# Two transformer-like layers on one core: expert work per block of 128 rows in two shared banks, two banks for the scores S, and an order offset for every step

## The chip, the cores and the metric

The kernel runs on one core of one Trainium2 chip. The metric is the time of one launch on the device in microseconds (us). Three runs of the kernel before gave a median of 2736.35 us (2729.3 to 2741.03).

## The reference

The input x is 16 batches of 512 rows and 128 channels, all float32. Two layers follow each other; each computes a mixing part `s` and a gating part `g` and adds their product:

```
xn = layernorm(x)
x  = x + mix(xn) * silu(experts(xn))
```

In layer 0 the mixing part is an RWKV time mix: five small low-rank mixes, projections r, k, v, g, a decay w, a linear recurrence over 512 positions for 2 heads of 64 channels, a group norm and an output projection. The expert part picks the best 2 of 8 experts for each row and sums their outputs, weighted by a softmax:

```
h1 = x @ W1[e].T ; h2 = x @ W2[e].T          # 128 -> 256
y  = (h1 * sigmoid(h1) * h2) @ W3[e].T       # 256 -> 128
```

In layer 1 the mixing part is softmax attention over 512 positions with 16 heads of 8 channels. The expert part again picks 2 of 8 experts (the gate is a sigmoid, applied to the input rows) and adds a ninth expert, the shared one, that every row passes through.

## The kernel before

**Engines and order.** Each step of the computation is a tuple `(n, layer, kind, ...)` for batch n. `due_times()` (L138) writes a due time for each step of an even and an odd batch, in microseconds relative to the start of the batch; `due()` (L255) adds PERIOD = 150.23 for each batch. `order(engine)` (L333) sorts all steps by due time plus one offset for each engine and kind, `LATER` (L124). Each engine runs its part of each step in that order, strictly. A due time thus sets only the order; the time at which work runs is set by semaphores. The work of several batches and of both layers is interleaved in that one order.

**Experts.** Rows of two batches are sorted by expert into NB = 23 blocks of 128 rows. SP loads three weight tiles for each block (`weights`, into a ring of WRING = 4). TensorE (PE) transposes four blocks at a time (`xT`). A unit of work is a pair of blocks, one every UNIT_EVERY = 10.7 us of due time: `up` writes four 128x128 products (2 blocks x 2 halves of the hidden width) into bank h, `gate` four into bank g (L711 to L728), and `down` writes two products, each a sum over two halves, into bank y (L729 to L750). ScalarE (ACT) takes tanh of bank h (L984), VectorE (DVE) multiplies with bank h and then with bank g (L1329, L1337). After every second pair ACT copies bank y, four blocks, to SBUF in one instruction (`yout`, L992), and SP stores it. The shared expert is two units of 512 rows, one for each half of the hidden width: `up` and `gate` are each one matmul of 512 columns (L719). Its `down` is eight matmuls of 128 columns (L741) and ACT copies it out in one instruction (`shared`, L997).

**Attention.** For each of 16 heads and 4 query blocks, `smax` writes the scores S of 128 queries and 512 keys to bank s (L887), and DVE takes the row maximum (L1445). Later the transposed scores minus the maximum go to bank st (`soft`, L902), and ACT takes exp into `probs` (L1063). `pv` multiplies with v (L916). The bias rows of the keys, which add the maximum, come from the instruction that copies the keys (`keys`, L1046, with a bias column).

**PSUM.** There are eight banks of 128x512 float32: mix and attn (all other work of layer 0 and layer 1), h, g, y, s, st and pv. `room()` makes PE wait until the bank that it is about to fill has been emptied, `content()` makes a reader wait until it has been filled.

```
            def room(s, b, i=0):
                if fill(s, b, i) > 1:
                    pe.wait_ge(emptied[b], fill(s, b, i) - 1)
                return bank[b]
```

**POOL** does elementwise work of layer 0 and the indirect DMAs that scatter rows to blocks and gather them back. It is not edited, but its order is.

Of the kernel before, what the change touches and what calls it, by code (L numbers as in the profile page):

```python
# [23 lines left out]
F32 = mybir.dt.float32  # L24
# [3 lines left out]
ALU = mybir.AluOpType  # L28
# [22 lines left out]
PAIRS, QUADS = (NB + 1) // 2, (NB + 3) // 4  # L51
HALF, FIRST = (PAIRS + FT) // 2, 8
# [31 lines left out]
GATE_AFTER = 3.13  # L84
DOWN_AFTER = 9.35
# [38 lines left out]
LATER = {'dve': {'keys': -0.95, 'decays': -1.98, 'gate': 0.4, 'norm': -0.45, 'weights': -0.86, 'cross128': -0.06, 'soft': -0.63, 'xT': 1.23, 'down': -2.14, 'mrow': 0.36, 'cross512': -0.24, 'scatter': -1.18, 'combine': -0.18, 'fetch': 0.58, 'outT': -0.02, 'yout': -0.28, 'value': 0.32, 'up': 0.06, 'decay': 0.75, 'finish': 0.7, 'wkvsum': 0.41, 'attnv': -3.03, 'normx': 0.61, 'yn': -0.01, 'diag': 0.22, 'proj': 0.52, 'shared': -0.39, 'pair': -1.16, 'cross256': -2.03, 'normT': 1.49, 'gather': 0.51, 'qk': -0.52, 'wkvT': 0.16, 'stack': 0.68, 'place': -0.69, 'mixed': 0.23, 'smax': -0.5, 'rank': -0.55, 'wkv': 0.06, 'weigh': -0.09, 'lora': -0.01, 'route': -0.07, 'mixin': -0.02, 'headsT': -0.17, 'pv': 0.53}, 'act': {'combine': -2.74, 'finish': 0.06, 'norm': -0.45, 'normx': -1.63, 'wkvT': 0.51, 'decay': 0.05, 'place': -1.66, 'outT': 0.85, 'down': -1.04, 'mrow': 0.28, 'normT': 0.35, 'route': 0.83, 'weights': -0.01, 'rank': 1.59, 'decays': -0.17, 'value': -0.08, 'lora': 1.09, 'wkv': -0.19, 'pair': -0.92, 'scatter': 1.57, 'smax': -2.19, 'cross256': -1.14, 'level': -2.39, 'mixed': 0.75, 'gate': 1.56, 'weigh': -0.63, 'headsT': 1.65, 'keys': 0.0, 'fetch': 0.93, 'cross128': 0.52, 'wkvsum': 1.0, 'yout': -0.63, 'shared': -0.22, 'attnv': 0.09, 'yn': -0.68, 'stack': 0.23, 'mixin': -0.02, 'gather': 0.09, 'diag': 1.25, 'cross512': -0.29, 'proj': 0.48, 'up': -0.0, 'xT': -0.03}, 'pool': {'xT': -0.33, 'combine': 0.06, 'cross512': -1.35, 'yn': -0.4, 'decay': -1.18, 'normx': -0.81, 'wkvT': 0.01, 'place': -0.48, 'attnv': 0.31, 'cross128': -0.93, 'fetch': -0.7, 'shared': 1.29, 'gate': 0.02, 'proj': -2.38, 'up': -1.17, 'mrow': -1.39, 'pv': -1.28, 'decays': -0.35, 'cross256': -0.02, 'qk': -0.22, 'soft': -0.4, 'diag': 1.02, 'lora': 1.06, 'stack': -0.02, 'yout': 0.94, 'weights': 1.23, 'mixed': -1.93, 'route': -0.07, 'mixin': -1.35, 'normT': -0.75, 'rank': 0.28, 'down': -1.25, 'finish': -0.92, 'scatter': -1.12, 'wkvsum': 0.13, 'outT': 0.11, 'pair': 0.13, 'norm': -0.24, 'smax': -2.87, 'level': -0.19, 'keys': 0.14, 'weigh': -0.21, 'wkv': -1.48, 'value': -0.18, 'gather': -0.21}, 'pe': {'wkvT': 0.16, 'outT': 0.36, 'decay': 0.03, 'cross512': -1.89, 'decays': 0.61, 'pv': 0.31, 'normx': -2.94, 'cross256': -0.05, 'gather': 0.77, 'proj': -0.06, 'down': -1.15, 'xT': -0.05, 'pair': 0.29, 'norm': 0.32, 'lora': -0.74, 'cross128': -0.29, 'mixin': 2.35, 'headsT': 0.35, 'place': 1.83, 'yout': 0.68, 'combine': 1.77, 'soft': -0.04, 'weigh': -1.08, 'fetch': -1.68, 'wkvsum': -0.26, 'normT': 0.17, 'mixed': 0.21, 'gate': -0.06, 'yn': 0.7, 'up': -0.14, 'value': -0.74, 'keys': 1.89, 'diag': 0.74, 'qk': 0.02, 'attnv': -0.64, 'rank': -0.03, 'shared': -0.84, 'mrow': 0.17, 'route': 0.18, 'wkv': -0.79, 'weights': 2.03, 'scatter': -0.45, 'finish': -0.51, 'level': -0.32}, 'sp': {'smax': 0.64, 'pv': -0.29, 'attnv': -0.42, 'scatter': 0.19, 'xT': -0.1, 'place': -1.05, 'headsT': 1.02, 'normx': 0.27, 'yout': 1.14, 'normT': -0.09, 'level': -0.3, 'yn': 0.57, 'cross256': 2.02, 'combine': 0.02, 'rank': -0.15, 'cross128': 0.28, 'wkvsum': 0.6, 'fetch': 0.14, 'soft': 0.62, 'weights': -0.11, 'qk': 0.85, 'weigh': 0.25, 'decays': 0.36, 'wkvT': 0.24, 'outT': -0.0, 'up': 1.39, 'diag': 0.2, 'wkv': -1.04, 'gate': -0.07, 'route': -2.12, 'mixin': 0.01, 'keys': 1.3, 'stack': -1.16, 'gather': 0.66, 'value': -1.01, 'mrow': -0.13, 'lora': -0.04, 'pair': -0.13, 'shared': -0.03, 'mixed': 0.26, 'proj': -0.33, 'down': 0.15, 'cross512': 0.17}}  # L124


def pair_of(layer, u):

    return u - FT * layer if u >= FT * layer else None


def blocks_of(layer, u):

    p = pair_of(layer, u)
    return list(range(2 * p, min(2 * p + 2, NB)))


def due_times():  # L138
# [33 lines left out]
    for i in range(4 * HALF):  # L172
        at = UNIT_START + UNIT_EVERY * i
        j = i % (2 * HALF)
        if FIRST <= j < FIRST + FT:
            unit(odd if i < 2 * HALF else even, 1, j - FIRST, at + (PERIOD if i < 2 * HALF else 0.0))
        else:
            layer = int(i >= 2 * HALF)
            unit(even, layer, (j if j < FIRST else j - FT) + FT * layer, at + 2 * PERIOD * layer)
# [23 lines left out]
def unit(d, layer, u, at):  # L203

    d[layer, "up", u] = at
    d[layer, "gate", u] = at + GATE_AFTER
    p = pair_of(layer, u)
    if p is not None or u == FT - 1:
        d[layer, "down", u] = at + DOWN_AFTER
    if p is None:  # L210
        if u == FT - 1:
            d[1, "shared"] = d[1, "down", u] + YOUT_AFTER
        return
    for b in blocks_of(layer, u):
        d[layer, "weights", b] = at - WEIGHTS_BEFORE + 0.3 * (b % 2)
    if p % 2 == 0:
        d[layer, "xT", p // 2] = at - XT_BEFORE
    if p % 2 or p == PAIRS - 1:
        d[layer, "yout", p // 2] = at + DOWN_AFTER + YOUT_AFTER

# [24 lines left out]
HB, GB, YB, SB, TB, VB = "h", "g", "y", "s", "st", "pv"  # L245
BANKS = MISC + (HB, GB, YB, SB, TB, VB)
# [5 lines left out]
EXPERTS = ("weights", "xT", "up", "gate", "down", "yout", "shared")  # L252


def due(step):  # L255
# [19 lines left out]
    return PERIOD * n + at  # L275


def fills(step):

    n, layer, kind, *which = step  # L280
    if kind in ("up", "gate"):
        return [HB if kind == "up" else GB]
    if kind == "down":
        p = pair_of(layer, which[0])
        return [YB] if p is None or p % 2 == 0 else []
    if kind in ("smax", "soft"):

        if n == 0 and kind == "smax" and which[0] < HG and which[1] % 2:
            return [TB]
        if n == B - 1 and kind == "soft" and which[0] % 2:  # L290
            return [SB if which[0] >= NH - HG else MISC[0]]
        return [SB if kind == "smax" else TB]
    if kind == "pv":
        return [VB] if which[1] == 0 else []
    if kind in ("keep", "load", "mixed", "norm", "decays", "weights", "yout", "shared", "scatter", "fetch", "gather", "combine", "normx", "weigh", "place", "yn", "keys"):
        return []
    return [MISC[layer]] * (2 if kind in ("mixin", "decay") else 1)
# [3 lines left out]
UPS = [s for s in PLAN if s[2] == "up"]  # L301
DOWNS = [[s for s in PLAN if s[1:3] == (i, "down")] for i in (0, 1)]
# [20 lines left out]
def down_of(s):  # L323

    n, layer, _, u = s
    return (n, layer, "down", FT - 1 if pair_of(layer, u) is None else u)


def quad_fill(n, layer, m):

    return fill((n, layer, "down", 2 * m + FT * layer), YB)


def order(engine):

    return sorted(PLAN, key=lambda s: due(s) + LATER[engine].get(s[2], 0.0))


def two_layer_kernel(nc, x, cols, mix1, square, mix2, dec1, dec2, up0, gate0, down0, up1, gate1, down1,
                     routers, ident, masks, select, iota, out):  # L340
    with ExitStack() as ctx:
# [69 lines left out]
        hid = sb("hid", [P, HRING, T])  # L411
# [118 lines left out]
        th_done = sem("th_done")  # L530
        down_done = [sem(f"down_done{i}") for i in L]
# [25 lines left out]
        def _(sp):  # L557
# [62 lines left out]
            def weights(s):  # L620
# [5 lines left out]
                if i >= WRING:  # L626

                    old = LOADS[i - WRING]
                    down = (old[0], old[1], "down", old[3] // 2 + FT * old[1])
# [6 lines left out]
            def yout(s):  # L636
# [3 lines left out]
                sp.wait_ge(emptied[YB], quad_fill(n, layer, m))  # L640
# [10 lines left out]
        def _(pe):  # L651
# [23 lines left out]
            def step(s):  # L675
# [38 lines left out]
                elif kind in ("up", "gate"):  # L714
                    u, part = which[0], 0 if kind == "up" else 1
                    b = HB if kind == "up" else GB
                    if pair_of(layer, u) is None:
                        pe.wait_ge(emptied[MISC[1]], fill((n, 1, "normT"), MISC[1]))
                        mm(room(s, b)[:], shared_sb[:, part, u * P:(u + 1) * P], xnT1[:], start=True, stop=True).then_inc(filled[b], 1)  # L719
                    else:  # L720
                        ps = room(s, b)
                        for i, blk in enumerate(blocks_of(layer, u)):
# [8 lines left out]
                elif kind == "down":  # L731
# [4 lines left out]
                    if p is None or p % 2 == 0:  # L736
                        room(s, YB)
# [872 lines left out]
```

## Time and profile before

| What | Value |
|---|---|
| median of 3 runs | 2736.35 us |
| lowest and highest run | 2729.3 and 2741.03 us |
| span of the profiled execution | 2756.3 us |
| PE busy (matmuls) | 2327.5 us, 84% |
| PE busy (weight loads) | 1579.5 us, 57% |
| DVE busy | 1609.7 us, 58% |
| ACT busy | 1350.3 us, 49% |
| POOL busy | 1237.6 us, 45% |
| mean granted TensorE clock | 0.946 |

The profiled execution has no time of its own beside its span, from first to last instruction; that span is 20 us above the median of the runs, which were not profiled. Matmuls are pipelined and the profile models their ends, so that a matmul is counted busy for longer than it keeps the next one from starting: two matmuls of one queue overlap in the list. The weight loads (PEld) are a second row of the same engine.

### The profile page before, as it was taken

What the parts mean: (1) busy time and instruction counts of PE and PEld (TensorE: products, weight loads), DVE (VectorE), ACT (ScalarE), POOL (GpSimd) and SP (SyncE); (2) the same over time, 40 slices, a digit from 0 to 9 for tenths busy, and PEclk for the clock granted to TensorE, in tenths of its full rate; (3) what the DMA queues carried; (4) which work ended last, traced back from release to release, by engine and by line L of the source; (5) the groups of instructions that cost most, each with busy time, mean ns of one, the idle gap of its engine ahead of it and who ended that gap; (6) DMA issues with size and microseconds to landing.
All of it is one profiled execution on the core that took longest, in us unless ns stands there. A gap on an engine that the chain in (4) does not pass through costs nothing. (4 is left out here: it accounts for less than half of the span.)

```text
span 2756.3 us, 50388 instructions
## 1 busy us (share of the span) xinstructions
PE 2327.5 (84%) x16602; PEld 1579.5 (57%) x16602; DVE 1609.7 (58%) x3864; ACT 1350.3 (49%) x2485; POOL 1237.6 (45%) x1364
## 2 busy tenths in 40 slices
PE   1666889898998989898898989889898889998785
PEld 1553556566665656566565656556565656665363
DVE  2336465766657475665657465665647566665452
ACT  0222555455554546545554545545554555555453
POOL 3144435364633645444732646435643646323503
PEclk5768899999999999999999999999999999999897
DMA  3320223323333333323332333324333332321132
GB/s 104 111 75 12 68 91 95 106 73 111 98 100 89 99 99 99 94 77 111 101 103 82 99 93 97 107 75 121 100 90 93 96 102 85 110 72 41 53 107 68
DMA packets 308767, 248.27 MB, mean 90 GB/s; under 512 B 31040, under 2 KB 300064, under 8 KB 308512
## 3 DMA queue, kind: packets, MB, share of 16 engines
q1 hardware_dynamic: 292128, 211.46, 25.7%
q0 software_dynamic: 16384, 33.59, 4.1%
q8 instruction: 138, 2.26, 0.3%
q14 instruction: 117, 0.96, 0.1%
HBM read 195.77 MB, written 48.10 MB: 88 GB/s over the span
## 5 line engine op out<-in xcount | busy, mean ns | idle before, releaser
L1445 DVE TENSOR_REDUCE rowmax<-bank_s 128x1 f32<-128x512 f32 x1016 | 698.5, 687 | 565.6 <-PE bank_s L887 542.3
L1063 ACT ACTIVATE probs<-bank_st 128x512 f32<-128x512 f32 x992 | 589.4, 594 | 462.7 <-PE bank_st L902 431.9
L902 PE MATMUL bank_st<-qs,ks 128*128 128x512 f32 x992 | 512.6, 517 | 59.3 <-ACT probs L1063 58.0
L887 PE MATMUL bank_s<-ks,qs 128*128 128x512 f32 x1016 | 448.6, 442 | 93.8 <-DVE rowmax L1445 84.9
L1207 POOL DMA_INDIRECT yg<-ys_d,index x256 | 249.8, 976 | 260.7 <-issue 242.1
L902 PEld LDWEIGHTS bank_st<-qs,ks 128*128 128x128 f32 x992 | 191.5, 193 | 234.5 <-ACT probs L1063 140.6
L887 PEld LDWEIGHTS bank_s<-ks,qs 128*128 128x128 f32 x1016 | 197.0, 194 | 207.4 <-DVE rowmax L1445 173.6
L1329 DVE SCALAR_TENSOR_TENSOR hid<-hid,bank_h 128x512 f32<-128x512 f32 x224 | 148.6, 664 | 223.7 <-ACT hid L984 216.7
L916 PE MATMUL bank_pv<-probs,v 128*32 128x512 f32 x2048 | 253.8, 614 | 0.8 <-ACT probs L1063 0.8
L728 PEld LDWEIGHTS bank_h<-xT_sb,wbuf 128*128 128x128 f32 x1472 | 202.6, 202 | 27.9 <-issue 14.6
L1125 POOL TENSOR_TENSOR pause_sb<-ones_sb,power_sb 128x8 f32<-128x8 f32 x128 | 214.2, 1674 | 3.9
L728 PE MATMUL bank_h<-xT_sb,wbuf 128*128 128x128 f32 x1472 | 211.7, 288 | 4.6 <-DMA wbuf<-down 2.4
L728 PEld LDWEIGHTS bank_g<-xT_sb,wbuf 128*128 128x128 f32 x1472 | 195.0, 195 | 30.7 <-issue 20.0
L747 PEld LDWEIGHTS bank_y<-wbuf,hid 128*128 128x128 f32 x1472 | 193.8, 193 | 23.8 <-DVE hid L1337 7.1
L1146 POOL TENSOR_TENSOR xmixT<-moved,xnT 128x512 f32<-128x512 f32 x80 | 86.9, 1086 | 264.2 <-DVE moved L1367 259.7
L747 PE MATMUL bank_y<-wbuf,hid 128*128 128x128 f32 x1472 | 199.6, 278 | 4.2 <-DVE hid L1337 4.1
L728 PE MATMUL bank_g<-xT_sb,wbuf 128*128 128x128 f32 x1472 | 200.9, 279 | 0.0
L984 ACT ACTIVATE hid<-bank_h 128x512 f32<-128x512 f32 x224 | 130.2, 581 | 130.4 <-PE bank_h L728 121.7
L1046 ACT ACTIVATE ks<-bank_attn,cols_sb 32x512 fp32r<-32x512 f32 x256 | 173.7, 679 | 16.0 <-PE bank_attn L879 13.1
L1133 POOL TENSOR_TENSOR rstd<-vareps,power_sb 128x4 f32<-128x4 f32 x32 | 32.5, 1015 | 316.5 <-DVE vareps L1288 316.5
L1337 DVE TENSOR_TENSOR hid<-hid,bank_g 128x512 f32<-128x512 f32 x224 | 148.0, 661 | 28.7 <-PE bank_g L728 13.6
L1195 POOL DMA_INDIRECT xs_d<-xn,index x128 | 127.3, 995 | 61.7 <-DVE index L1555 31.6
(245 smaller groups left out, 3659.4 us busy)
## 6 DMA issues: line engine op xcount, KB each, us to landing
wbuf<-up SPq DMA_DIRECT2D x368, 128.0 KB
wbuf<-gate SPq DMA_DIRECT2D x368, 128.0 KB
wbuf<-down SPq DMA_DIRECT2D x368, 128.0 KB
xs_sb<-xs_d SPq DMA_DIRECT2D x80, 256.0 KB
ys_d<-y_sb SPq DMA_DIRECT2D x80, 256.0 KB
xn<-x SPq DMA_DIRECT2D x16, 256.0 KB, 3.2
x<-x SPq DMA_DIRECT2D x16, 256.0 KB, 4.1
yg<-ys_d,index POOLq DMA_INDIRECT x256
```

The lines of the kernel that those rows point to most:

```text
L728: last = mm(ps[:, (FT * i + f) * P:(FT * i + f + 1) * P], wbuf[:, load % WRING, part, f * P:(f + 1) * P], rows, start=True, stop=True)
L747: last = mm(bank[YB][:, blk % 4 * P:(blk % 4 + 1) * P], hid[:, NUMBER[n, layer, "up", u] % HRING, (FT * i + f) * P:(FT * i + f + 1) * P], ...
L887: mm(room(s, b)[:], qs[:, slot, q * P:(q + 1) * P], ks[:, slot, j, :], start=True, stop=True).then_inc(filled[b], 1)
L902: mm(room(s, b)[:], ks[:, slot, j, k * P:(k + 1) * P], qs[:, slot, :], start=True, stop=True).then_inc(filled[b], 1)
L916: last = mm(ps[32 * j:32 * j + 32, :], v1_all[:, k, (DK + 1) * (HG * g + j):(DK + 1) * (HG * g + j) + VCOLS], probs[:, slot, :], start=k = ...
L1046: last = A(ks[rows, (NG * n + g) % RING, j, :], content((n, 1, "stack", AK, g), misc)[rows, :], ACT.Identity, bias=cols_sb[rows, COL_KONE: ...
L1063: A(probs[:, tile % PRING, :], ps[:], ACT.Exp).then_inc(emptied[b], 1)
L1125: tt(pause_sb[:], ones_sb[:].to_broadcast([P, 8]), power_sb[:], ALU.pow).then_inc(rested, 1)
L1207: pool.indirect_dma_start(yg[layer][:, k, q, :], None, ys_d[layer][:, :], where).then_inc(gathered[layer], 16)
L1329: v.scalar_tensor_tensor(out=hid[:, i % HRING, 0:wide], in0=hid[:, i % HRING, 0:wide], scalar=1.0, in1=bank[HB][:, 0:wide], op0=ALU.add, o ...
L1337: v.tensor_tensor(hid[:, i % HRING, 0:wide], hid[:, i % HRING, 0:wide], ps[:, 0:wide], ALU.mult).then_inc(emptied[GB], 1)
L1445: v.reduce_max(rowmax[:, h // HG % 2, NT * (h % HG) + q:NT * (h % HG) + q + 1], content(s, b)[:], AX).then_inc(emptied[b], 1)
```

## The change

1. The expert unit is one block, one every 5.35 us of due time. Its `up` step writes all four products, up and gate, into one bank (columns 0 to 255 and 256 to 511). Its `down` step writes into the first 128 columns of the same bank once DVE has read both parts. Units take the banks e0 and e1 in turn. ACT copies each block's 128x128 result to SBUF by itself; `yout` is only the store. The shared expert becomes four units of 128 rows in the same form.
2. Banks h, g, y and s become e0, e1, s0 and s1. S alternates between s0 and s1 by query block.
3. `MOVED` adds an offset to each single step of a pair of batches (with further offsets for the first two and the last two batches), and `SHIFTED` an offset for each engine, layer and kind. `GATE_AFTER`, `DOWN_AFTER` and some entries of `LATER` change.
4. The bias rows of the keys are set to 1.0 once, by four memsets at the start. The key copies take 24 rows instead of 32 and have no bias column.

```diff
-GATE_AFTER = 3.13
-DOWN_AFTER = 9.35
+GATE_AFTER = 1.5
+DOWN_AFTER = 6.5
...
+        for k in range(2):
+            if first + k < NB + SHARED * layer:
+                unit(d, layer, first + k, at + k * UNIT_EVERY / 2)
...
-HB, GB, YB, SB, TB, VB = "h", "g", "y", "s", "st", "pv"
+EB, SB, TB, VB = ("e0", "e1"), ("s0", "s1"), "st", "pv"
...
-    return PERIOD * n + at
+    return PERIOD * n + at + moved(step)
+
+MOVED = (
+    {
+        (0, 0, "combine"): [0.23], (0, 0, "cross128"): [-2.17], (0, 0, "cross256"): [1.4], (0, 0, "cross512"): [0, -0.58], (0, 0, "decay"): [-2.67],
...
+        (0, 0, "yout"): [2.72, 1.08, -1.22, 0, -6.42, -14.1], (0, 1, "attnv"): [-0.49], (0, 1, "combine"): [0.39],
...
+def moved(step):
+    n = step[0]
+    i, still = PLACES[n % DUO][step[1:]]
+    return DRIFT * n + among(MOVED, n, (n % DUO, *step[1:3]), i, still)
+
+def shifted(engine, step):
+    every, *ends = SHIFTED[engine].get(step[1:3], (0, 0, 0))
+    return every + (ends[class_of(step[0]) - 1] if class_of(step[0]) else 0)
...
+    if kind in ("up", "down"):
+        return [EB[TURN[n, layer, which[0]] % 2]]
...
-        return [SB if kind == "smax" else TB]
+        return [SB[which[1] % 2] if kind == "smax" else TB]
...
 def order(engine):
-    return sorted(PLAN, key=lambda s: due(s) + LATER[engine].get(s[2], 0.0))
+    return sorted(PLAN, key=lambda s: due(s) + LATER[engine].get(s[2], 0.0) + shifted(engine, s))
...
+                    ps = room(s, b)
+                    for part in range(2):
+                        for f in range(FT):
+                            last = mm(ps[:, (FT * part + f) * P:(FT * part + f + 1) * P], w[:, part, f * P:(f + 1) * P], rows,
+                                      start=True, stop=True)
+                    last.then_inc(up_done, 1)
                 elif kind == "down":
...
+                    ps = room(s, b)
+                    for f in range(FT):
+                        last = mm(ps[:, 0:P], hid[:, turn_of(n, layer, u) % HRING, f * P:(f + 1) * P], w[:, 2, f * P:(f + 1) * P],
+                                  start=f == 0, stop=f == FT - 1)
                     last.then_inc(down_done[layer], 1)
...
+                    act.wait_ge(up_done, i + 1)
...
+                    A(hid[:, i % HRING, :], bank[fills(s)[0]][:, 0:FT * P], ACT.Tanh, scale=0.5).then_inc(th_done, 1)
+                elif kind == "down":
+                    act.wait_ge(down_done[layer], NUMBER[s] + 1)
...
+                    A(dst, bank[b][:, 0:P], ACT.Copy).then_inc(emptied[b], 1)
...
-                    rows = slice(32 * j, 32 * j + 32)
-                    last = A(ks[rows, (NG * n + g) % RING, j, :], content((n, 1, "stack", AK, g), misc)[rows, :], ACT.Identity,
-                             bias=cols_sb[rows, COL_KONE:COL_KONE + 1])
+                    rows = slice(32 * j, 32 * j + 3 * DK)
+                    last = A(ks[rows, (NG * n + g) % RING, j, :], content((n, 1, "stack", AK, g), misc)[rows, :], ACT.Copy)
...
+                    for j in range(HG):
+                        v.memset(ks[32 * j:32 * j + 32, :, j, :].bitcast(F32), 1.0).then_inc(s_late, 1)
```

## Rows read from the trace of the kernel before

**Rows 1.** The page: busy time and share of each engine.
```profile
PE 2327.5 (84%) x16602; PEld 1579.5 (57%) x16602; DVE 1609.7 (58%) x3864; ACT 1350.3 (49%) x2485; POOL 1237.6 (45%) x1364
```

**Rows 2.** The steady stretch as one window: busy us (instructions) of each engine.
```profile
450.00:2400.00 1950.00, 1742.56 (x12873) 1197.51 (x12871) 1232.12 (x2951) 1038.94 (x1922) 947.57 (x1040) 0.99 0.33 97
```

**Rows 3.** PE's waits, whole span: releaser, us in total, times, longest.
```profile
PE bank_s L887 <- DVE rowmax L1445: 84.9, 129, 1.8
PE bank_st L902 <- ACT probs L1063: 58.0, 102, 2.6
```

**Rows 4.** PE's waits within 450 to 2400 us.
```profile
PE bank_s L887 <- DVE rowmax L1445: 58.5, 88, 1.6
PE bank_st L902 <- ACT probs L1063: 39.7, 71, 0.8
```

**Rows 5.** Waits of the weight loads of the same two lines, whole span.
```profile
PEld bank_s L887 <- DVE rowmax L1445: 173.6, 257, 2.3
PEld bank_st L902 <- ACT probs L1063: 140.6, 201, 3.0
PEld bank_st L902 <- issue: 83.4, 163, 1.7
PEld bank_s L887 <- issue: 16.0, 53, 0.8
```

**Rows 6.** Timeline near 1207 us: start, duration, engine, instruction, idle before.
```profile
1207.07 0.39 PE L887 MATMUL bank_s<-ks,qs 128*128 128x512 f32 x1
...
1207.50 0.69 DVE L1445 TENSOR_REDUCE rowmax<-bank_s 128x1 f32<-128x512 f32 x1 [0.44 <-PE bank_s L887]
...
1207.92 0.63 PE L902 MATMUL bank_st<-qs,ks 128*128 128x512 f32 x1
1208.24 0.19 PEld L887 LDWEIGHTS bank_s<-ks,qs 128*128 128x128 f32 x1
1208.39 0.40 PE L887 MATMUL bank_s<-ks,qs 128*128 128x512 f32 x1
```

**Rows 7.** Timeline of PE: a 512-column matmul (two passes), then four 128-column ones.
```profile
1201.61 1.02 PE L719 MATMUL bank_g<-xnT,shared_sb 128*128 128x512 f32 x2
1202.07 0.80 PE L902 MATMUL bank_st<-qs,ks 128*128 128x512 f32 x1
...
1226.72 1.05 PE L747 MATMUL bank_y<-wbuf,hid 128*128 128x128 f32 x8
1227.53 0.48 PE L902 MATMUL bank_st<-qs,ks 128*128 128x512 f32 x1
```

**Rows 8.** Groups by line and form: the shared expert's first matmuls.
```profile
L719 PE MATMUL bank_h<-xnT,shared_sb 128*128 128x512 f32 x64 | 33.5, 605 | 0.0
```

**Rows 9.** Groups of ACT by form: busy us, mean ns, then idle before.
```profile
L1046 ACT ACTIVATE ks<-bank_attn,cols_sb 32x512 fp32r<-32x512 f32 x256 | 173.7, 679 | 16.0 <-PE bank_attn L879 13.1 <-issue 0.2
L984 ACT ACTIVATE hid<-bank_h 128x512 f32<-128x512 f32 x208 | 124.1, 597 | 127.8 <-PE bank_h L728 119.2 <-PE bank_h L719 6.0
L992 ACT ACTIVATE y_sb<-bank_y 128x512 f32<-128x512 f32 x80 | 47.3, 591 | 20.4 <-PE bank_y L747 18.9 <-issue 1.5
...
L1039 ACT ACTIVATE qs<-bank_attn 128x512 fp32r<-128x512 f32 x64 | 38.2, 597 | 63.8 <-PE bank_attn L879 59.0 <-issue 4.7
...
L984 ACT ACTIVATE hid<-bank_h 128x256 f32<-128x256 f32 x16 | 6.1, 381 | 2.6 <-PE bank_h L728 2.5
L1105 ACT ACTIVATE expd<-cum 128x128 f32<-128x128 f32 x16 | 4.8, 302 | 0.0
```

**Rows 10.** Groups of DVE by form: one expert product at two widths.
```profile
L1329 DVE SCALAR_TENSOR_TENSOR hid<-hid,bank_h 128x512 f32<-128x512 f32 x208 | 142.1, 683 | 218.5 <-ACT hid L984 211.5 <-issue 7.0
...
L1329 DVE SCALAR_TENSOR_TENSOR hid<-hid,bank_h 128x256 f32<-128x256 f32 x16 | 6.6, 411 | 5.2 <-ACT hid L984 5.2
```

**Rows 11.** Timeline of the start: the memset of the keys, and PE's wait.
```profile
106.99 5.18 DVE L1296 MEMSET ks<- 128x6144 f32 x1 [1.23 <-issue]
...
118.78 1.08 PE L712 MATMUL bank_mix<-ident_sb,xs_sb 128*128 128x128 f32 x4 [7.85 <-DVE moved L1367]
```

More of the change, by code:

```diff
@@ L138, in due_times, with block_of @@
+def block_of(layer, u):
+    return u - SHARED * layer if u >= SHARED * layer else None
 def due_times():
@@ L206, in unit @@
     d[layer, "gate", u] = at + GATE_AFTER
[L207 to L212, printed above, removed]
-        return
[L214 to L219, printed above, removed]
+    d[layer, "down", u] = at + DOWN_AFTER
+    b = block_of(layer, u)
+    if b is None:
+        return
+    d[layer, "weights", b] = at - WEIGHTS_BEFORE
+    if b % 4 == 0:
+        d[layer, "xT", b // 4] = at - XT_BEFORE
+    if b % 4 == 3 or b == NB - 1:
+        d[layer, "yout", b // 4] = at + DOWN_AFTER + YOUT_AFTER
 def attention(d, start):
@@ L251 @@
 PLACED_IN = ("route", "weigh", "place", "rank", "scatter", "fetch")
-EXPERTS = ("weights", "xT", "up", "gate", "down", "yout", "shared")
+EXPERTS = ("weights", "xT", "up", "gate", "down", "yout")
 def due(step):
@@ new lines, in class_of, with among @@
+def class_of(n):
+    return 1 if n < DUO else 2 if n >= B - DUO else 0
+def among(table, n, key, i, otherwise):
+    at = table[0].get(key, otherwise)[i]
+    return at + table[class_of(n)].get(key, otherwise)[i] if class_of(n) else at
+PLACES = [{} for i in range(DUO)]
+for places, steps in zip(PLACES, DUE):
+    for s in sorted(steps):
+        kin = [t for t in sorted(steps) if t[:2] == s[:2]]
+        places[s] = (kin.index(s), [0.0] * len(kin))
+def moved(step):
+    n = step[0]
+    i, still = PLACES[n % DUO][step[1:]]
+    return DRIFT * n + among(MOVED, n, (n % DUO, *step[1:3]), i, still)
@@ L290, in fills @@
         if n == B - 1 and kind == "soft" and which[0] % 2:
-            return [SB if which[0] >= NH - HG else MISC[0]]
-        return [SB if kind == "smax" else TB]
+            return [SB[0] if which[0] >= NH - HG else MISC[0]]
+        return [SB[which[1] % 2] if kind == "smax" else TB]
     if kind == "pv":
         return [VB] if which[1] == 0 else []
-    if kind in ("keep", "load", "mixed", "norm", "decays", "weights", "yout", "shared", "scatter", "fetch", "gather", "combine", "normx", "weigh", "place", "yn", "keys"):
+    if kind in ("keep", "load", "mixed", "norm", "decays", "weights", "gate", "yout", "scatter", "fetch", "gather", "combine", "normx", "weigh", "place", "yn", "keys"):
@@ L301 @@
 UPS = [s for s in PLAN if s[2] == "up"]
+TURN = {(s[0], s[1], s[3]): i for i, s in enumerate(UPS)}
 DOWNS = [[s for s in PLAN if s[1:3] == (i, "down")] for i in (0, 1)]
@@ L320, in fill, with turn_of @@
     return BEFORE[step, bank] + n + 1
[L323 to L331, printed above, removed]
+def turn_of(n, layer, u):
+    return TURN[n, layer, u]
 def order(engine):
-    return sorted(PLAN, key=lambda s: due(s) + LATER[engine].get(s[2], 0.0))
+    return sorted(PLAN, key=lambda s: due(s) + LATER[engine].get(s[2], 0.0) + shifted(engine, s))
 def two_layer_kernel(nc, x, cols, mix1, square, mix2, dec1, dec2, up0, gate0, down0, up1, gate1, down1,
@@ L639, in yout @@
                 i, count = NUMBER[s], min(4, NB - 4 * m)
-                sp.wait_ge(emptied[YB], quad_fill(n, layer, m))
+                last = (n, layer, "down", min(4 * m + 3, NB - 1) + SHARED * layer)
+                sp.wait_ge(emptied[fills(last)[0]], fill(last, fills(last)[0]))
                 if n > 0 and m == 0:
@@ L713, in step @@
                     last.then_inc(filled[misc], 1)
[L714 to L717, printed above, removed]
+                elif kind == "up":
+                    u = which[0]
+                    blk, b = block_of(layer, u), fills(s)[0]
+                    if blk is None:
                         pe.wait_ge(emptied[MISC[1]], fill((n, 1, "normT"), MISC[1]))
-                        mm(room(s, b)[:], shared_sb[:, part, u * P:(u + 1) * P], xnT1[:], start=True, stop=True).then_inc(filled[b], 1)
+                        w, rows = shared_sb, xnT1[:, u * P:(u + 1) * P]
@@ L720, in step @@
                     else:
-                        ps = room(s, b)
-                        for i, blk in enumerate(blocks_of(layer, u)):
-                            load, turned = NUMBER[n, layer, "weights", blk], (n, layer, "xT", blk // 4)
-                            pe.wait_ge(w_in[load % WRING], 48 * (load // WRING + 1))
-                            pe.wait_ge(emptied[misc], fill(turned, misc))
-                            rows = xT_sb[:, NUMBER[turned] % 2, blk % 4 * P:(blk % 4 + 1) * P]
-                            for f in range(FT):
-                                last = mm(ps[:, (FT * i + f) * P:(FT * i + f + 1) * P], wbuf[:, load % WRING, part, f * P:(f + 1) * P], rows,
-                                          start=True, stop=True)
@@ L730, in step @@
-                        last.then_inc(filled[b], 1)
+                        load, turned = NUMBER[n, layer, "weights", blk], (n, layer, "xT", blk // 4)
+                        pe.wait_ge(w_in[load % WRING], 48 * (load // WRING + 1))
+                        pe.wait_ge(emptied[misc], fill(turned, misc))
+                        w, rows = wbuf[:, load % WRING], xT_sb[:, NUMBER[turned] % 2, blk % 4 * P:(blk % 4 + 1) * P]
+                    ps = room(s, b)
[3 more added lines that the diff above has]
+                                      start=True, stop=True)
@@ L731, in step @@
+                    last.then_inc(up_done, 1)
                 elif kind == "down":
                     u = which[0]
-                    pe.wait_ge(emptied[GB], fill((n, layer, "gate", u), GB))
-                    p = pair_of(layer, u)
-                    if p is None or p % 2 == 0:
-                        room(s, YB)
-                    if p is None:
-                        for q in range(NT):
-                            for f in range(FT):
-                                last = mm(bank[YB][:, q * P:(q + 1) * P], hid[:, NUMBER[n, 1, "up", f] % HRING, q * P:(q + 1) * P],
-                                          shared_sb[:, 2, f * P:(f + 1) * P], start=f == 0, stop=f == FT - 1)
-                    else:
-                        for i, blk in enumerate(blocks_of(layer, u)):
-                            load = NUMBER[n, layer, "weights", blk]
-                            for f in range(FT):
-                                last = mm(bank[YB][:, blk % 4 * P:(blk % 4 + 1) * P],
-                                          hid[:, NUMBER[n, layer, "up", u] % HRING, (FT * i + f) * P:(FT * i + f + 1) * P],
-                                          wbuf[:, load % WRING, 2, f * P:(f + 1) * P], start=f == 0, stop=f == FT - 1)
@@ L750, in step @@
+                    blk, b = block_of(layer, u), fills(s)[0]
+                    w = shared_sb if blk is None else wbuf[:, NUMBER[n, layer, "weights", blk] % WRING]
+                    ps = room(s, b)
+                    for f in range(FT):
+                        last = mm(ps[:, 0:P], hid[:, turn_of(n, layer, u) % HRING, f * P:(f + 1) * P], w[:, 2, f * P:(f + 1) * P],
+                                  start=f == 0, stop=f == FT - 1)
                     last.then_inc(down_done[layer], 1)
```

235 lines of the change are left out of this document (185 added, 50 removed).

## The prediction

> **What bounds the kernel now.** I read the busy shares first. PE is busy 84% of the span of 2756.3 us, DVE 58%, ACT 49%, POOL 45% [rows 1]: PE is the engine to watch, and nothing else is near full. The steady stretch comes next, since the span holds a start and an end that the change touches little: of its 1950 us PE is busy 1742.6, so 207 us are idle [rows 2]. The list of PE's waits then says who ends the idle time. The first entry is the score matmul S, held by the row maximum on DVE because S has one bank: 84.9 us in 129 waits. The second is the transposed score matmul, held by exp on ACT: 58.0 us in 102 [rows 3]. In the steady stretch the two are 58.5 and 39.7 us, 98 of 207; the remaining 109 is spread over dozens of pairs of instructions [rows 4].
>
> PE's idle time understates these waits, because a matmul is counted busy while its end drains. For one, S starts at 1207.07, the maximum runs from 1207.50 to 1208.19, the next weight load of S comes at 1208.24 and the matmul at 1208.39 [rows 6]. PE waited for DVE there, yet its row shows no idle time, since the matmul of 1207.92 is drawn until 1208.55. The weight loads' waits show the other side: 173.6 us in 257 for S, 140.6 us in 201 for the transposed scores [rows 5]. These hold the time in which PE is streaming anyway. Where the loads of the same lines wait for nothing, the gap is 16.0/53 = 0.30 us for S and 83.4/163 = 0.51 us for the other. Taken off, 173.6 - 257 x 0.30 = 97 us and 140.6 - 201 x 0.51 = 38 us remain.
>
> All sums are made against the span of 2756.3 us. The runs' median is 2736.35, 20 us or 0.7% lower, without a profiler; a difference of some tens of us carries over unchanged.
>
> **1. A second bank for S.** S(k) now waits for the maximum of k-2, not k-1, so each wait shrinks by the distance of two S steps; at 64 a batch and a due-time period of 150 us this is 2.35 us, and the longest wait was 1.8 us (2.3 at the load) [rows 3, 5]. Nearly all go. Bounds of the gain: 84.9 (idle alone) to 173.6 us (all of the loads' waits). I take 105, near the 97 worked out above, with a little for waits of other steps behind a late S.
>
> **2. What is late next.** The transposed scores keep one bank. In the order they mostly stand beside an S, so a PE that no longer stops at S reaches them earlier, while ACT is no faster. Nothing returned is one end, all 105 the other. I take a quarter, +25: an exp of 0.6 us is followed in the plan by 2.35 us to the next, so most of the time is still there, but 201 of the loads did wait [rows 5].
>
> **3. The shared expert in blocks.** Before, a batch had four float32 matmuls of 512 columns (64 records of bank h are 16 batches x 2 units x 2 passes [rows 8], bank g as many). After, it has 16 of 128 columns. Start to start, the 512-column one took 1202.07 - 1201.61 = 0.46 us; four of 128 columns took 1227.53 - 1226.72 = 0.81 us, 0.20 each; by their drawn length of 1.05 us it would be 0.26, and I take 0.22 [rows 7]. 16 x 0.22 - 4 x 0.46 = 1.7 us a batch, x 16 = +27 us, all on PE: the weights are loaded four times as often. Bounds: 0 (hidden in waits that stay) to +37 (at 0.26). The routed experts keep their number of matmuls, only grouped differently: 0, ends -5 and +5 by the gap of 0.30 at a load.
>
> A 128-column pass thus takes about 0.11 us [rows 7], about as long as the load of its weights would leave. The Trainium skill (TensorE: Matmul & The Clock Gate, Back-to-back issue gap) gives, for an isolated matmul at the full clock, N/2.4 + 2.5 ns, which is 56 ns at N=128 and 216 at N=512. By that, a pass four times as narrow costs a quarter, and the split would be nearly free (an estimate from the page: 32 x 56 against 8 x 216 ns, +0.1 us a batch). The trace disagrees for this stream, and the rows decide.
>
> **4. More and smaller instructions on ACT and DVE.** Units go from 14 a batch to 27 (46 routed and 8 shared in two batches), 432 in all. ACT: tanh before 208 x 0.597 + 16 x 0.381 = 130 us, after 432 x 0.381 = 165, +35. Copies out: 80 and 32 more, all taken at 0.591, make 66 us; after, 432 of 128x128, no such row, nearest is the narrow exp of 302 ns: 130, +64. Keys: 256 x (0.679 - 0.597) = -21, the nearest copy without a bias being that of the queries. Together +78 us on an engine with half its time free [rows 1, 9]. DVE: two products a unit, 448 of 0.68 become 864 of 0.41: +58 us [rows 10]. Both lie beside PE's work, which covers them; what shows is that an exp sometimes stands behind one more copy. Bounds 0 and +78, taken +10, as the idle of ACT is eight times the addition. If the cover fails, this becomes the rival below.
>
> **5. The unit's bank.** A bank is held from `up` until the copy after `down`. Work alone: 0.9 + 0.38 + 2 x 0.41 + 0.46 + 0.30 = 2.9 us; in due times 6.5 plus the down and its copy, 7.3 us, against 10.7 us until its next turn. Slack 3.4 us: cost 0, ends 0 and +43 (a tenth of a microsecond for each of 432). DVE used to read bank h while PE wrote bank g; now ACT's tanh waits until all four products are there, about 0.45 us later; that is within the slack. The Trainium skill (PSUM — Partial Sum Buffer, PSUM bank collisions raise a hardware error) says that two engines may not touch one bank at once and want a semaphore by bank. That is the rule against this layout, since four steps of three engines must now take turns in it; no row of before shows a bank shared so. What it costs in time would be the holding time just given.
>
> **6. The memsets.** Four of 1536 elements a row beside one of 6144 in 5.18 us: +5.2 us on DVE at about 115 us. It is on the path: PE stood 7.85 us for the product behind those memsets [rows 11]. +5, ends 0 and +5.2.
>
> **7. The order.** Single steps move by up to some 3 us against their neighbours, the last stores by more; PE's queue, DVE's, ACT's, POOL's gathers and scatters and SP's loads are all re-sorted. No instruction is added. The profile can't price it. It has two bounds: the 109 us of steady idle in other pairs [rows 2, 4] can be gained, or as much be lost. Since S, the exp of its neighbour and the units now stand at places chosen singly, bunches of them can be spread, which part 2 counts as a loss. I take -30, a quarter of the gain's end.
>
> **Sum.** -105 + 25 + 27 + 10 + 0 + 5 - 30 = -68 us. 2756 - 68 = 2688 of span, 2668 us as a run.
>
> **The rivals.** *The forecast* is 2610 to 2715, chance 0.52.
>
> *The order gains much more* (0.15). For: a mean wait of 0.56 to 0.66 us [rows 4] is of a size that moving one step by a few us can remove. Against: part 2 and real dependences within layer 0. All of S and the 109: -105 - 109 + 27 + 10 + 5 = -172, so 2564; half of the others 2618. I put it at 2590.
>
> *The bank was not the cause* (0.13). DVE is late because its strict order holds the maximum behind products that wait for ACT: 218 us of idle stand before the product of bank h [rows 10]. Then the second bank only moves the stop: parts 1 and 2 cancel, 27 + 10 + 5 - 30 = +12 remains, 2748; with a third of the gain kept, 2715. Around 2735. Against: the maximum itself mostly waits for PE, as in the pair above [rows 6].
>
> *ACT's queue blocks, slower* (0.20). Each of the 320 added copies out (432 - 112) stands in ACT's strict order and waits for its `down`, and exps stand behind it that free the bank PE wants. A blocked exp costs the copy's 0.30 and about 0.15 of waiting. If all hit, 320 x 0.45 = 144, and with part 1 wholly gained and no luck in the order: -105 + 25 + 27 + 5 + 144 = +96, 2832; two thirds of them make +48, 2784. It decides from (105 - 25 - 27 - 5) / 0.45 = 107 hits. For: ACT's exp already ends 102 waits of PE. Against: ACT is idle half the time. I put it at 2780.
>
> **How the numbers follow.** The likeliest case gives 2668; its own range is 2610 to 2715. To hold 8 in 10 the range leaves out half of the order's case below and most of the slower case above: 2590 to 2755. A change within 0.5% (2722.7 to 2750) is about what a measurement of this kernel cannot tell from none. Faster takes the forecast, the order's case and 0.04 of the third: 0.71. Same takes 0.09 of the third and 0.02 of the last: 0.11. Slower keeps 0.18.
>
> **What would show it.** Right: PE's wait of L887 for the maximum under 20 us instead of 84.9; the wait of the transposed scores at 65 to 90; the shared expert's passes 512 instead of 128, 0.11 us apart; ACT busy 1430 and DVE 1670 us; PE busy higher in share, idle in the steady stretch under 150 us. Wrong: an unchanged wait at S (third case), a wait at the transposed scores above 110 us or exps idle behind copies (last case), waits of the e banks in PE's list (part 5), or a span below 2630, which only the order could bring.

## The result, and the profile after

The kernel after takes 2510.48 us (median of 4 runs, 2507.8 to 2512.7), the kernel before 2732.82 us beside it. The ratio is 0.9189 with a 95% interval of 0.9166 to 0.9213, 222 us less. The forecast was 2668 us with a range of 2590 to 2755: the direction was right, the size was a third of the real one, and the result lies outside the range.

The page after, its first line of busy times, answers to [rows 1]:

```profile
span 2510.7 us, 51608 instructions
## 1 busy us (share of the span) xinstructions
PE 2243.5 (89%) x16986; PEld 1596.2 (64%) x16986; DVE 1623.3 (65%) x4284; ACT 1395.2 (56%) x3013; POOL 1247.4 (50%) x1364
```

The span is 246 us shorter. Work was added to PE (384 matmul passes), ACT (+45 us) and DVE (+14 us); what went is for the most part time in which engines waited. The steady stretch answers to [rows 2]: idle time of PE was 207 of 1950 us and is 84 of 1750 us.

```profile
450.00:2200.00 1750.00, 1665.67 (x12995) 1202.10 (x12996) 1231.49 (x3271) 1062.87 (x2303) 952.02 (x1034) 0.99 0.36 107
```

The gain is in the steady part. The first matmul of layer 0's mixing starts at 93.6 us in batch 0 and at 2400.5 us in batch 15 of the kernel before, that is 153.8 us a batch; after, the same instruction starts at 87.8 and 2188.2 us, 140.0 us a batch. Its line in the view by source line, before and after (durations in ns, then first and last start):

```profile
L753 PE MATMUL bank_mix<-xxxT,mix_sb x32: 592/697/1220, 93.6 to 2400.5; 128*128 128x512 f32 x32
```
```profile
L919 PE MATMUL bank_mix<-xxxT,mix_sb x32: 590/592/1222, 87.8 to 2188.2; 128*128 128x512 f32 x32
```

13.8 us in each of 15 batches is 207 of the 246 us. After batch 15's start the end is 33 us shorter, and the start 6 us.

PE's waits after, whole span, answer to [rows 3], the loads' to [rows 5]:

```profile
PE bank_st L1068 <- ACT probs L1228: 38.4, 84, 1.4
PE bank_mix L887 <- DMA xs_sb<-xs_d: 34.3, 1, 34.3
PE bank_mix L847 <- DVE kT L1582: 25.2, 10, 4.5
PE bank_e L914 <- DVE hid L1501: 17.8, 7, 14.4
...
PE bank_e L904 <- ACT y_sb L1163: 7.1, 17, 0.5
PE bank_s L1053 <- DVE rowmax L1610: 7.1, 14, 1.7
```
```profile
PEld bank_st L1068 <- ACT probs L1228: 101.1, 175, 1.9
...
PEld bank_s L1053 <- DVE rowmax L1610: 28.6, 45, 2.2
```

The wait at S fell from 84.9 to 7.1 us, as step 1 said. But the wait at the transposed scores fell too, from 58.0 to 38.4 us (140.6 to 101.1 at the loads), where step 2 had it grow. The wait for the e banks is 7.1 us. PE's idle time fell by 162 us (2756.3 - 2327.5 = 429, 2510.7 - 2243.5 = 267), the span by 246: the other 84 us came out of PE's busy time, though it has more instructions. For a good part that is the drawn end of matmuls, under which a wait hides: the same 992 matmuls of the transposed scores are drawn 53 us shorter. Their group, before and after (busy us, mean ns, then idle time before):

```profile
L902 PE MATMUL bank_st<-qs,ks 128*128 128x512 f32 x992 | 512.6, 517 | 59.3 <-ACT probs L1063 58.0 <-issue 0.7
```
```profile
L1068 PE MATMUL bank_st<-qs,ks 128*128 128x512 f32 x992 | 459.7, 463 | 38.9 <-ACT probs L1228 38.4
```

A small part is the clock. The mean granted TensorE clock rose from 0.946 to 0.953 of full speed. In the ten runs of the first experiment below it lies between 0.942 and 0.948, and the time falls by 1.6 us for each 0.001 of it (a straight line through the ten runs). By that the rise goes with about 11 of the 246 us. This is an estimate, and it doesn't say which of the two causes the other.

### The profile page after: what moved, and what is told of

The parts are those of the page before. It is cut to its first block and busy times, and to the rows that moved or that the text cites. A ratio compares the mean times of both kernels' runs of the same rounds, so it can differ in the third digit from the quotient of the medians.

```text
span 2510.7 us, 51608 instructions
## 1 busy us (share of the span) xinstructions
PE 2243.5 (89%) x16986; PEld 1596.2 (64%) x16986; DVE 1623.3 (65%) x4284; ACT 1395.2 (56%) x3013; POOL 1247.4 (50%) x1364
## 5 line engine op out<-in xcount | busy, mean ns | idle before, releaser
L1068 PE MATMUL bank_st<-qs,ks 128*128 128x512 f32 x992 | 459.7, 463 | 38.9 <-ACT probs L1228 38.4
L904 PEld LDWEIGHTS bank_e<-xT_sb,wbuf 128*128 128x128 f32 x2944 | 383.3, 193 | 60.1 <-issue 37.9
L904 PE MATMUL bank_e<-xT_sb,wbuf 128*128 128x128 f32 x2944 | 397.9, 279 | 11.0 <-ACT y_sb L1163 7.1
L1495 DVE SCALAR_TENSOR_TENSOR hid<-hid,bank_e 128x256 f32<-128x256 f32 x432 | 179.4, 415 | 232.3 <-ACT hid L1149 231.3
L1068 PEld LDWEIGHTS bank_st<-qs,ks 128*128 128x128 f32 x992 | 189.7, 191 | 169.9 <-ACT probs L1228 101.1
L914 PE MATMUL bank_e<-wbuf,hid 128*128 128x128 f32 x1472 | 232.1, 281 | 17.8 <-DVE hid L1501 17.5
L1149 ACT ACTIVATE hid<-bank_e 128x256 f32<-128x256 f32 x432 | 165.5, 383 | 143.6 <-PE bank_e L904 140.8
L914 PEld LDWEIGHTS bank_e<-wbuf,hid 128*128 128x128 f32 x1472 | 213.2, 194 | 49.1 <-DVE hid L1501 22.4
L1501 DVE TENSOR_TENSOR hid<-hid,bank_e 128x256 f32<-128x256 f32 x432 | 177.9, 412 | 4.4
L1163 ACT ACTIVATE y_sb<-bank_e 128x128 f32<-128x128 f32 x368 | 101.7, 276 | 121.0 <-PE bank_e L914 116.0
L1212 ACT ACTIVATE ks<-bank_attn 24x512 fp32r<-24x512 f32 x256 | 150.3, 587 | 7.0 <-PE bank_attn L1045 4.0
L1360 POOL DMA_INDIRECT xs_d<-xgate,index x128 | 131.6, 1028 | 33.9 <-POOL xgate L1354 26.4
```

Of the source, the lines that this page charges most:

```text
L904: last = mm(ps[:, (FT * part + f) * P:(FT * part + f + 1) * P], w[:, part, f * P:(f + 1) * P], rows, start=True, stop=True)
L914: last = mm(ps[:, 0:P], hid[:, turn_of(n, layer, u) % HRING, f * P:(f + 1) * P], w[:, 2, f * P:(f + 1) * P], start=f == 0, stop=f == FT - 1)
L1068: mm(room(s, b)[:], ks[:, slot, j, k * P:(k + 1) * P], qs[:, slot, :], start=True, stop=True).then_inc(filled[b], 1)
L1360: pool.indirect_dma_start(xs_d[layer][:, :], where, src, None).then_inc(scattered0 if layer == 0 else scattered1[piece % GRING], 16)
L1495: v.scalar_tensor_tensor(out=hid[:, i % HRING, :], in0=hid[:, i % HRING, :], scalar=1.0, in1=bank[fills(s)[0]][:, 0:FT * P], op0=ALU.add, ...
L1501: v.tensor_tensor(hid[:, i % HRING, :], hid[:, i % HRING, :], bank[b][:, FT * P:2 * FT * P], ALU.mult).then_inc(emptied[b], 1)
```

## The experiments

All times are medians; each has its own runs of the kernel before beside it (2732.6 to 2735.1 us). Differences are taken to 2510.5 us or to the experiment named. They hold what the granted clock did as well. By the 1.6 us above, that is under a fifth of each difference of 100 us or more, but for the ones in experiments 6 and 9 where it is named.

**1. Without the offsets of single steps, with two banks and with one.**

```diff
 def moved(step):
...
+    return 0.0
 def shifted(engine, step):
...
+    return 0.0
```

(`DRIFT`, which `moved` also adds, is 0 in the kernel.)

> The kernel after with moved() and shifted() returning 0: block units and two S banks stay, each step stands where its due time and the offset by engine and kind put it. Theory A (the two S banks took the stops away, and the order only tidies up): 2560 to 2620 us, S waits of PE under 20 us. Theory B (the place of each single step is worth most of the 222 us): 2680 us or more, with the waits spread over many pairs of instructions.

2726.3 us, ratio 0.9979 (0.9966 to 0.9991): nearly the whole gain is gone.

```diff
-        return [SB[which[1] % 2] if kind == "smax" else TB]
+        return [SB[0] if kind == "smax" else TB]
```

> As no_offsets, and S in one bank again. What is left of the change is the unit of one block and the key copies. Theory A: 120 us or more above no_offsets, near 2740 us, S waits of PE back at 85 us. Theory B: at most 40 us above no_offsets.

2837.2 us, ratio 1.0377 (1.0354 to 1.0401). So with the old kind of order the second bank is worth 111 us net, where steps 1 and 2 together had 105 - 25 = 80. The unit of one block, with the rest of the change, costs 104 us against the kernel before, where steps 3, 4 and 6 had 42. This rest includes that the entries of `up`, `gate` and `down` in `LATER`, up to 2.14 us in the kernel before, are 0 now. And the offsets are worth 2726.3 - 2510.5 = 216 us, where step 7 had 30. Both theories had part of it: B had the place of the gain, and A was near the worth of the bank (120 or more). PE's waits without offsets, two banks and then one:

```profile
PE bank_st L1068 <- ACT probs L1228: 83.2, 155, 2.7
```
```profile
PE bank_s L1053 <- DVE rowmax L1610: 98.9, 145, 3.0
PE bank_st L1068 <- ACT probs L1228: 66.1, 127, 2.7
```

Step 2 holds here: with the second bank, the wait at the transposed scores goes from 66.1 to 83.2 us.

**2. Offsets at half size.** `moved` and `shifted` return half.

> The kernel after with all offsets of single steps and of engines and kinds at half their size. Theory A: within 15 us of 2510 us, since the order hardly matters. Theory B: halfway between the kernel after and no_offsets, 2590 us or more.

> As two_s_05, with S in one bank. It prices the second bank under another order. Theory A: 120 us or more above two_s_05. Theory B: less than 40 us above it.

Two banks 2623.9 us (0.9602, 0.9583 to 0.9622), one bank 2827.4 us (1.0344, 1.0320 to 1.0367). Half the offsets give 102 of the 216 us with two banks and 10 us with one. The bank is worth 203 us here. Theory A's condition for this run (120 or more) holds and B's does not, while for the two-bank run it is the other way round. Neither theory had that each part needs the other.

**3. All offsets, one bank in 7 of 8 groups of heads.**

```diff
+        return [(SB[which[1] % 2] if (n % DUO, which[0] // HG) in [(1, 1)] else SB[0]) if kind == "smax" else TB]
```

> The kernel after with all its offsets, S in one bank in 7 of the 8 groups of heads of a pair of batches (the order of the eighth cannot run with one bank). If the bank's worth grows with the order, as from 111 us without offsets to 203 us at half size, it is 250 us or more here: 2740 us or above, with S waits of PE above 200 us. If it is worth what it is without offsets: 2610 us.

2790.5 us, ratio 1.0209 (1.0180 to 1.0238): 280 us above the kernel after. With one bank the full offsets give at most 47 us (2837.2 to 2790.5), with two 216. The cause stands in the waits of this kernel:

```profile
PE bank_s L1053 <- DVE rowmax L1610: 227.7, 304, 3.8
...
PE bank_st L1068 <- ACT probs L1228: 12.9, 29, 1.1
```

The wait for exp is nearly gone in it and the wait for the row maximum is 227.7 us. We read it so: in this order S is what PE does instead of waiting for exp, and with one bank it waits for the row maximum instead.

**4. What the second bank permits.** The timeline after, near 1027 us (start, duration, engine):

```profile
1026.63 0.39 PE L1053 MATMUL bank_s<-ks,qs 128*128 128x512 f32 x1
1026.86 0.60 PE L914 MATMUL bank_e<-wbuf,hid 128*128 128x128 f32 x4
1026.88 0.59 ACT L1228 ACTIVATE probs<-bank_st 128x512 f32<-128x512 f32 x1
1027.06 0.69 DVE L1610 TENSOR_REDUCE rowmax<-bank_s 128x1 f32<-128x512 f32 x1 [0.59 <-PE bank_s L1053]
...
1027.22 0.48 PE L1053 MATMUL bank_s<-ks,qs 128*128 128x512 f32 x1
...
1027.54 0.48 PE L1068 MATMUL bank_st<-qs,ks 128*128 128x512 f32 x1
...
1027.86 0.44 PE L1053 MATMUL bank_s<-ks,qs 128*128 128x512 f32 x1
1027.99 0.68 DVE L1610 TENSOR_REDUCE rowmax<-bank_s 128x1 f32<-128x512 f32 x1
1028.06 0.60 ACT L1228 ACTIVATE probs<-bank_st 128x512 f32<-128x512 f32 x1 [0.28 <-PE bank_st L1068]
1028.14 1.05 PE L904 MATMUL bank_e<-xT_sb,wbuf 128*128 128x128 f32 x8
```

Three S steps start within 1.23 us while DVE takes one maximum; the second starts at 1027.22 while the maximum of the first runs until 1027.75. With one bank the second would have had to wait for that. Counting S in PE's timeline from 450 to 2200 us, starts under 1.0 us behind the last one are 0 before, 9 without offsets and 123 after (41 more stand in one row with their neighbour). The next two runs take the offsets of S and of the transposed scores away alone (`moved` returns 0 for that kind).

> The kernel after with the single-step offsets of the S steps at zero, so that S stands evenly, one every 2.35 us of due time; all other offsets stay. All attention offsets together were worth 104 us. If PE gains by taking S steps in pairs where it would otherwise stop: 40 us or more slower, 2550 us and above, and far fewer S starts under 1.0 us apart. If the places of the transposed scores carry it: within 15 us of 2510 us.

> The mirror: the single-step offsets of the transposed scores at zero, S keeps its own. If the S pairs carry the gain: within 20 us of 2510 us. If the places of the transposed scores do: 2550 us and above, with PE's waits for exp above 60 us instead of 38 us.

Without S's own places 2549.6 us (0.9324, 0.9309 to 0.9340), +39; the starts under 1.0 us fall to 94, and PE's wait at S is 31.3 us instead of 7.1. Without those of the transposed scores 2519.8 us (0.9218, 0.9202 to 0.9233), +9, and their wait is 30.4 us, not above 60. S's places matter more, but they are 39 of the 216 us. The count of close pairs fell less than expected; that other offsets still bunch them is likely and not shown.

**5. Whose offsets.** Offsets zero for attention, then for the expert steps, then for both.

> The kernel after with the offsets of all attention steps (stack, keys, smax, mrow, soft, pv, headsT, qk, attnv, outT) at zero; experts and layer 0 keep theirs. If the gain of 216 us comes from spreading S and its neighbours: 2680 us or more. If from where the expert units stand against each other and layer 0: 2560 us or less.

> The kernel after with the offsets of the expert steps (weights, xT, up, gate, down, yout) at zero; attention and layer 0 keep theirs. The mirror of not_attention: if the attention's places carry the gain, below 2580 us; if the experts' do, above 2650 us. If both are above 2620 us, the offsets only work together.

> The kernel after with offsets only for the steps that are neither attention nor expert units (layer 0's mixing, norms, routing, scatter, gather, combine). Attention's offsets were worth 104 us and the experts' 74 us when each was taken away alone; of the 216 us of all, 38 remain. If the parts add up: 2688 us. If they only work together (the sum of the losses is larger than the whole): 2715 us or more. If these steps matter more than the rest leaves them: 2660 us or less.

2614.9 us (0.9561, 0.9532 to 0.9589), 2584.0 us (0.9444, 0.9417 to 0.9471) and 2660.4 us (0.9747, 0.9725 to 0.9770). Losses: attention 104, experts 74, both together 150; the rest alone gains 66 of 216 (2726.3 to 2660.4). No one group carries it. The two losses add up to 178 and are 150 together, so the groups overlap a little rather than need each other.

**6. Does PE's work set the time?** First PE leaves out half of the shared expert's `up` step (the gate products), then it does the other half twice:

```diff
-                    for part in range(2):
+                    for part in range(1 if blk is None else 2):
```
```diff
-                    for part in range(2):
+                    for part in ((0, 0, 1) if blk is None else (0, 1)):
```

> The kernel after with the gate half of the shared expert's products left out of PE's work (the second part of the matmuls of its up step; the rest, and all instructions of the other engines, stay). 256 passes of 128 columns less. If a pass on a nearly full PE costs its 0.11 us start to start: 28 us less, near 2482 us, and the split of the shared expert (384 passes more, 0.46 us instead of 0.88 us per matmul) cost the 27 us of the prediction. If PE's waits swallow it: within 8 us of 2510 us.

> The kernel after with the up half of the shared expert computed twice on PE, 256 more passes of 128 columns, results unchanged. If PE bounds the kernel: +28 us, 2538 us. If PE has slack there, as the run with 256 fewer passes suggests: within 8 us. If fewer passes gave nothing only since waits took their place, but more passes add: 2525 us or more.

256 passes less: 2510.5 us (0.9182, 0.9162 to 0.9201), no change. 256 more: 2525.7 us (0.9244, 0.9229 to 0.9260), +15. PE was 89% busy, and 28 us less of its work gave nothing. Two things took its place. The wait at the transposed scores grew:

```profile
PE bank_st L1068 <- ACT probs L1228: 48.5, 92, 2.5
```

From 38.4 to 48.5 us: it seems that the next exp was not earlier, so PE came to it sooner and stood. And the granted clock was lower, 0.948 to 0.951 in the five runs against 0.953 to 0.957 in the kernel after; with more passes it was 0.956 to 0.958. By the 1.6 us for each 0.001, that is about 8 us lost in the first run and 3 us won in the second (an estimate). At an equal clock, then, 28 us less work would give some 8 us and 28 us more would cost some 18. So PE's work sets a part of the time, at some 0.3 to 0.6 of its own length; for the rest the time is set by the sequence of PE, ACT and DVE.

**7. The key copies of before.**

> The kernel after with the key copies of before: 32 rows, Identity with a bias column. ACT gets 256 x 0.09 = 23 us of work back. If ACT is covered by PE: within 5 us of 2510 us. If exps behind the keys hold PE up at bank st: 10 us or more slower.

2509.2 us (0.9188, 0.9172 to 0.9205): no difference. ACT's 26 us more (1421.0 against 1395.2 busy) are covered.

**8. The memsets earlier.**

```diff
-                if s == (0, 0, "decay"):
+                if s == UPS[0]:
                     v.memset(ks[:].bitcast(F32), 0.0).then_inc(s_late, 1)
```

> The kernel after with all nine late memsets of DVE (keys, selection, row maxima, v) ahead of its first expert product instead of at layer 0's first decay step, in the idle time of DVE before 75 us. The trace after shows PE idle for 14.4 us at 103 to 118 us behind them. If that stop is on the path: 8 to 15 us faster than 2510 us, near 2498 us. If the work after it waits for something else anyway: within 4 us.

2498.8 us (0.9145, 0.9123 to 0.9167), 12 us below the kernel after: the best version here. After, PE's stop behind the memsets is

```profile
117.91 1.22 PE L914 MATMUL bank_e<-wbuf,hid 128*128 128x128 f32 x4 [14.43 <-DVE hid L1501]
```

and with the memsets in DVE's idle time at 41 to 56 us the same product waits 0.54 us:

```profile
103.92 0.71 PE L914 MATMUL bank_e<-wbuf,hid 128*128 128x128 f32 x4 [0.54 <-DVE hid L1501]
```

**9. Why single blocks without offsets are 104 us slower.** From one_s_no_offsets: the two blocks of a pair 1.0 us apart instead of 5.35, and `down` at 8.5 us instead of 6.5.

> one_s_no_offsets (2837 us: one bank for S, no offsets, units of one block) with the two blocks of a former pair placed 1.0 us apart in due time instead of 5.35 us, as the pair of before stood together. one_s_no_offsets is 104 us above the kernel before. If that loss is the order that suits pairs and not single blocks: 40 us or more faster than 2837 us. If it is in the unit itself (more passes, more instructions, shared banks): as slow or slower.

> one_s_no_offsets (2837 us) with down placed 8.5 us behind up instead of 6.5 us. If PE, ACT and DVE stop in the unit's chain because down and its copy stand too close behind the products: 20 us or more faster. If the loss of 104 us is not there: within 15 us, or slower as the bank is held longer.

2979.0 us (1.0897, 1.0871 to 1.0922) and 2879.1 us (1.0528, 1.0510 to 1.0545): both slower, by 142 and 42 us. With `down` later, PE waits for the e banks:

```profile
PE bank_e L904 <- ACT y_sb L1163: 33.9, 60, 1.2
```

That wait was 5.4 us in one_s_no_offsets:

```profile
PE bank_e L904 <- ACT y_sb L1163: 5.4, 12, 0.5
```

The slack of step 5, 3.4 us in due times, holds at 6.5 us; at 8.5 us 1.4 would be left, and it no longer covers. In the paired run the granted clock was 0.892 to 0.897 against 0.931 to 0.939. By the 1.6 us for each 0.001 about 67 of its 142 us go with that (an estimate); the rest is still a loss. So neither standing the blocks together nor a later `down` brings back any of the 104 us. Neither run restores the old places of the unit, though: `GATE_AFTER` 3.13, `DOWN_AFTER` 9.35 and the old entries of `LATER` were not tried. What makes up the 104 us stays open. By experiments 6 and 7 extra passes and copies explain a part of it at most, but these were measured in the other order.

## Why the prediction was wrong

**Step 1, the second bank, right in kind and low in the old order.** With what step 2 gives back, 80 us were forecast net and 111 measured without offsets. It was priced for one order only; its worth is 203 us at half offsets and about 280 at full ones.

**Step 2, returned at the transposed scores, right in sign without offsets** (+17 us in PE's list against 25), and wrong for the kernel after, where that wait fell by 20 us instead of growing to the 65 to 90 us that were named as a sign.

**Steps 3 and 4, the added work.** 27 us for the shared expert came from durations, as if PE's work were the time. Per pass the runs give 0 to 0.06 us, not 0.11 (0.03 to 0.07 at an equal clock, by the estimate in experiment 6); for the 384 passes added, 0 to 27 us. ACT is busy 1395 us instead of the 1430 forecast, DVE 1623 instead of 1670 (the narrow copies take 276 ns, not 302; the products took the forecast 0.41 us); the keys show no effect. Step 4 calls ACT's idle time eight times the addition; (2756 - 1350) / 78 is eighteen, which only strengthens it. The trace after has the narrow passes as long as step 3 had them, eight in at most 0.98 us:

```profile
1207.74 1.05 PE L904 MATMUL bank_e<-xT_sb,wbuf 128*128 128x128 f32 x8
1208.72 0.64 PE L1082 MATMUL bank_pv<-probs,v 128*32 128x512 f32 x4
```

The formula weighed in step 3 (the Trainium skill, TensorE: Matmul & The Clock Gate, Back-to-back issue gap) is that section's gap of an isolated matmul. For a sustained stream the same section gives about 81 ns at N=128 and 131 ns at N=512. By these the split costs 32 x 81 - 8 x 131 = 1544 ns a batch, about 25 us in all (an estimate from that section of the skill), near the term of 27 rather than near nothing. The traces have 101 to 123 ns from start to start for a pass of 128 columns (0.81 / 8 before, 0.98 / 8 after), above the 56 and the 81 ns. Yet all parts together, with the `LATER` entries of the unit at 0, cost 104 us. So the sum of parts 3 to 6, 42 us, was too small in that order.

**Step 5, the unit's bank, right.** PE waits 7.1 us for the copies that free it. Letting the engines take turns at one bank, as the Trainium skill (PSUM — Partial Sum Buffer, PSUM bank collisions raise a hardware error) wants it, cost PE no more than that in this trace.

**Step 6, the memsets, a little small.** 5 us forecast; the stop grew by 6.6 us, from 7.85 to 14.43, but taking all memsets away from there gives 12 us, which the forecast had not looked for.

**Step 7, the order, is the step that failed.** It said -30, of 109 us at most, the idle time outside S and the transposed scores. The runs gave -216. The bound itself was wrong in two ways. It counted idle time as PE's list shows it, though the first part of the prediction had just shown that a matmul's drawn end hides waits (84 us of the 246 came out of PE's busy time, a good part of them in such ends). And it gave the order only waits that steps 1 and 2 had not claimed, when the order and the bank act on the same ones: with two banks PE can take an S early while an exp runs, and an order that puts S steps there makes use of it. Of 327 us from one_s_no_offsets to the kernel after, 111 are the bank alone, at most 47 the order alone, and at least 169 only both. That the close S steps are how the two work together is shown for a part: S's own places are worth 39 us. Which places carry the rest stays open.

Two smaller errors partly cancelled, by luck: the unit cost 62 us more than steps 3, 4 and 6 had, and the bank gave 31 us more than steps 1 and 2 had.

The rival that named the order (0.15, 2590 us) had the right term and two thirds of the gain (146 of 222 us). It kept the bound of 109 us and did not have the bank and the order working together. The sign for it, a span below 2630, did come. The slower rival, ACT's queue, did not show.

## What to carry to other kernels

When a resource (a bank, a buffer) is added together with a new order, don't price them one after the other: ask what the order can do with it that it could not do before. The listed idle time is no bound on what a new order can give, since a busy row can hide a wait: here 216 us came where 109 were listed. And an engine at 89% busy does not thereby set the whole time: leave out some of its work, add some, see how far the time moves each way, and read the granted clock beside it.

## What the runs showed that was not expected

Taking 256 matmul passes of 0.11 us each off the busiest engine changed nothing, while adding as many cost 15 us. The granted clock moved with the work, down by 0.005 on average with less work and up by 0.002 with more, so part of what less work could have given went with a slower clock. And `down` placed 2 us later, with the stores and gathers whose due times follow from it, cost 42 us, 1.5% of the time, in an otherwise equal kernel.
